# Two stages of a two-layer gated cross-attention program: normalised tiles turned by transposing DMAs in place of TensorE transposes

## The reference, cut to what matters

```python
def _layernorm(x, axis=-1, eps=1e-05):
    m = jnp.mean(x, axis=axis, keepdims=True)
    v = jnp.var(x, axis=axis, keepdims=True)
    return (x - m) / jnp.sqrt(v + eps)
```

## Time and profile before

| | us |
|---|---|
| runs | 2868.49, 2858.22, 2860.1 |
| median | 2860.1 |
| span of the profiled execution | 2840.7 |
| shared stage, within the span | 483 to 1000, about |
| last stage, within the span | 1995 to 2841, about |

### The profile page before, as it was taken

One profiled execution on the slowest core, in us unless ns is written; L12 is line 12 of the kernel. 1 busy time (PEld: TensorE's weight loads), 2 busy tenths in 40 slices (PEclk: granted clock), 3 DMA queues, 4 the chain that ended last, 5 costly groups with the idle time before them and its releaser, 6 DMA issues. The chain is left out here.

```text
span 2840.7 us, 47238 instructions
## 1 busy us (share of the span) xinstructions
PE 2697.2 (95%) x18014; PEld 1530.0 (54%) x18014; DVE 1632.8 (57%) x2693; ACT 1484.6 (52%) x3650; POOL 1042.2 (37%) x823
## 2 busy tenths in 40 slices
PE   6999988999999999999999989999999999999999
PEld 4555544444444467777777655566444444444444
DVE  7888885755555456655665478887633423333232
ACT  4888885333223256666666479999433222332221
POOL 2445452375455646666666401111102201220111
PEclk9999999999999999999999989999999999999999
DMA  4011104211111279999999710101400000000000
GB/s 156 21 55 50 50 16 146 67 46 49 49 49 35 75 253 293 273 289 287 283 288 293 177 60 31 61 31 50 144 34 1 30 30 30 1 30 30 15 1 30
DMA packets 152320, 277.75 MB, mean 98 GB/s; under 512 B 20000, under 2 KB 28960, under 8 KB 152096
## 3 DMA queue, kind: packets, MB, share of 16 engines
q1 hardware_dynamic: 115232, 207.39, 20.7%
q0 software_dynamic: 36864, 67.34, 11.2%
HBM read 198.86 MB, written 75.89 MB: 97 GB/s over the span
## 5 line engine op out<-in xcount | busy, mean ns | idle before, releaser
L1424 POOL DMA_INDIRECT ids<-sh_tk,sh_su x256 | 269.8, 1054 | 245.6 <-PE sh_gu L55 87.9
L55 PE MATMUL ex_gu<-ex_xT,ex_h 128*128 128x256 f16 x3072 | 347.3, 273 | 1.7 <-ACT ex_xT L1697 1.7
L55 PEld LDWEIGHTS ex_gu<-ex_xT,ex_h 128*128 128x128 f16 x3072 | 301.1, 98 | 51.0 <-ACT ex_xT L1697 1.9
L1829 POOL DMA_INDIRECT xp<-ex_oo,ex_to x128 | 241.8, 1889 | 177.5 <-ACT ex_oo L1731 136.3
L2408 POOL TENSOR_TENSOR fe_prodT<-fe_pp,fe_prodT 128x512 f16<-128x512 f32 x64 | 76.8, 1199 | 604.4 <-ACT fe_prodT L2175 604.4
L533 PE MATMUL at_g<-id,at_p 128*128 128x128 f32 x1280 | 211.8, 290 | 43.7 <-POOL at_p L928 23.7
L1555 DVE SCALAR_TENSOR_TENSOR ex_h<-ring,ex_h 128x1024 f16<-128x1024 f32 x128 | 151.1, 1222 | 151.6 <-ACT ex_h L1545 151.6
L533 PEld LDWEIGHTS at_g<-id,at_p 128*128 128x128 f32 x1280 | 165.6, 170 | 114.3 <-issue 46.7
L701 ACT ACTIVATE at_s<-at_s,at_mx 128x154 f32<-128x154 f32 x512 | 210.3, 416 | 0.0
L927 POOL TENSOR_TENSOR at_p<-at_s,at_rs 128x1024 f32<-128x1024 f32 x64 | 121.5, 1899 | 234.2 <-DVE at_rs L826 234.2
L2319 DVE SCALAR_TENSOR_TENSOR ring<-fe_g,fe_nf,ring 128x512 f32<-128x512 f32 x32 | 24.0, 751 | 293.1 <-PE fe_g L2079 293.1
(11 more groups left out here) (355 smaller groups left out, 5679.9 us busy)
## 6 DMA issues: line engine op xcount, KB each, us to landing
ring<-L_ffn_expert_gate_up_w SPq DMA_DIRECT2D x64, 1024.0 KB, 7.9
ring<-L_ffn_expert_down_w SPq DMA_DIRECT2D x64, 512.0 KB, 8.9
ring<-x SPq DMA_DIRECT2D x24, 1024.0 KB, 5.8
x<-ring SPq DMA_DIRECT2D x16, 1024.0 KB, 5.1
zrows<-hm_zs SPq DMA_DIRECT2D x32, 256.0 KB, 2.0
xp<-ring SPq DMA_DIRECT2D x8, 1024.0 KB, 5.1
out<-ring SPq DMA_DIRECT2D x8, 1024.0 KB, 4.2
ring<-xp SPq DMA_DIRECT2D x7, 1024.0 KB, 5.6
```

The lines of the kernel that those rows point to most:

```text
L55: mm = nc.tensor.matmul(out, lhs(a, k), rhs(b, k), start=start and i == 0 and j == 0, stop=stop and i == n - 1 and j == 2)
L1424: e.indirect_dma_start(ids, bass.IndirectOffsetOnAxis(slotu[b % 2][:, t, j:j + 1], 0), pair[b % 2][:, t, j, :], None, bounds_check=SLOTS - ...
L1829: e.indirect_dma_start(dst, bass.IndirectOffsetOnAxis(to[:, n:n + 1], 0), o32[y % 2][:, t, :], None, bounds_check=T + SLOTS - 1, oob_is_er ...
```

## The change

In the shared and the last stage, and for the four tiles that the first attention prepares for the shared stage, a DMA of SP's queue turns the tile: `sync_turn` waits for the low half and issues one transposing DMA from the buffer `zs` (128 rows by 2 x 512 values of 16 bits) straight into the tile's part of `zT`, both in SBUF. Its 8 TensorE transposes and the eviction by ScalarE or VectorE are gone, and so are the turns' PSUM banks. A buffer is free for the next high half when the DMAs of the tiles of its parity in the block before have landed (`hi_freed`). Whoever reads a block waits for 32 on each of two semaphores. The two attentions turn their own tiles as before. In SP's queue the turns of block b + 1 stand ahead of the stores to `zrows` of the same tiles; in the last stage behind the load of block b + 2 and ahead of the wait for block b's finished rows. Each has a wait on the last reader of the `zT` buffer ahead of it. The diff, cut to its core (the lines left out take the same turns out of ScalarE's and VectorE's loops, and name the new class in the last stage):

```diff
@@ -148,12 +148,15 @@
         v.tensor_scalar(self.z[n % 2][:, :], self.block(b)[:, t, :], self.mv[:, t, 0:1], self.rstd[:, t:t + 1],
                         ALU.subtract, ALU.mult).then_inc(s["z"], 1)
 
+    def hi_freed(self, n):
+        return self.s["turned"], n - self.nzs + 1
+
     def scalar_high(self, n):
 
         a, s = self.nc.scalar, self.s
         a.wait_ge(s["z"], n + 1)
         if n >= self.nzs:
-            a.wait_ge(s["turned"], n - self.nzs + 1)
+            a.wait_ge(*self.hi_freed(n))
         a.copy(self.zs[n % self.nzs][:, 0, :], self.z[n % 2][:, :]).then_inc(s["hi"], 1)
 
     def vector_low(self, n):
@@ -196,6 +199,37 @@
 
         self.nc.tensor.wait_ge(self.s["even"], 2 * b + 2)
         self.nc.tensor.wait_ge(self.s["odd"], 2 * b + 2)
+
+
+class QueueNorm(Norm):
+
+
+
+    def tile_out(self, n):
+        return super().tile_out(n).rearrange("p h k n -> p (h k) n")
+
+    def hi_freed(self, n):
+        return self.pair_turned(n // TPB - 1, n % 2)
+
+    def sync_turn(self, n):
+
+        e, s, slot = self.nc.sync, self.s, n % self.nzs
+        e.wait_ge(s["lo"], n + 1)
+        e.dma_start_transpose(self.tile_out(n), self.zs[slot][:, :, :].rearrange("p h d -> p (h d)")
+                              ).then_inc(s["odd" if n % 2 else "even"], 16)
+
+    def pair_turned(self, b, odd):
+
+        return self.s["odd" if odd else "even"], 32 * (b + 1)
+
+    def turned_all(self, engine, b):
+
+        for odd in range(2):
+            engine.wait_ge(*self.pair_turned(b, odd))
+
+    def tensor_block(self, b):
+
+        self.turned_all(self.nc.tensor, b)
 
 
 def place(h):
...
@@ -545,7 +579,7 @@
                     mm.then_inc(s["k_mm"], 1)
 
             def piece(what, B, k):
-                if what == "turn":
+                if what == "turn" and B < NB:
                     nm, _, n = whose(B, k)
                     nm.tensor_turn(n, bank(("turn", B, k), nm.turn_out(n)))
                 elif what == "project":
@@ -634,8 +668,6 @@
             if maps_ahead:
                 e.wait_ge(s["expd"], 2 * UNITS - 1)
                 maps_ahead.tensor_first()
-            if rows_ahead:
-                e.wait_ge(rows_ahead.s["turned"], TPB)
             e.wait_ge(s["f_mm"], TPB * NB)
 
         def scalar():
@@ -653,7 +685,7 @@
                                  ).then_inc(s["w_hi"], 1)
                 elif what == "prepare":
                     nm.scalar_high(n)
-                elif what == "turn" and n % 2 == 0:
+                elif what == "turn" and B < NB and n % 2 == 0:
                     if B:
                         e.wait_ge(s["q_mm"], KT * B)
                     nm.scalar_turned(n, bank_of["turn", B, k])
@@ -730,7 +762,6 @@
                 e.wait_ge(maps_ahead.s["w_hi"], 2)
             if rows_ahead:
                 e.wait_ge(rows_ahead.s["w_hi"], 3)
-                e.wait_ge(rows_ahead.s["even"], 2)
 
         def vector():
             e = nc.vector
@@ -754,7 +785,7 @@
                     nm.vector_z(n)
                 elif what == "low":
                     nm.vector_low(n)
-                elif what == "turn" and n % 2:
+                elif what == "turn" and B < NB and n % 2:
                     if B:
                         e.wait_ge(s["q_mm"], KT * B)
                     nm.vector_turned(n, bank_of["turn", B, k])
...
@@ -955,6 +985,10 @@
                     if L0:
                         e.wait_ge(s["lim_got"], B)
                         mask(B)
+                elif what == "turn" and B == NB:
+                    if k == 0:
+                        e.wait_ge(s["q_mm"], KT * B)
+                    rows_ahead.nrm.sync_turn(k)
                 elif what == "finish" and k == TPB - 1:
                     if rows_ahead and B == NB - 1:
                         rows_ahead.sync_next()
@@ -983,7 +1017,7 @@
             for what in plan[-1]:
                 piece(*what)
             for n in range(STEPS):
-                for what in plan[n]:
+                for what in sorted(plan[n], key=lambda what: what[0] != "turn"):
                     piece(*what)
 
         own_steps = count(1)
@@ -1008,7 +1042,7 @@
     def __init__(self, nc, ctx, K, I, ring, s, src, homes):
         self.nc, self.I, self.s, self.src, self.homes = nc, I, s, src, homes
         self.x = [ring[i] for i in (3, 2, 4, 1, 0)]
-        self.nrm = Norm(nc, ctx, "sh", s, K, self.x, homes)
+        self.nrm = QueueNorm(nc, ctx, "sh", s, K, self.x, homes)
         self.slots = [ring[i] for i in (4, 1, 0)]
 
         self.scat = [ctx.enter_context(nc.semaphore(f"sh_scat{i}")) for i in range(2)]
...
@@ -1172,8 +1201,6 @@
                     mm.then_inc(s["gu_mm"], 1)
                     if b == 0 and f == 3:
                         positions(0)
-                    for t in turning(b, f) if b + 1 < NB else ():
-                        turn((b + 1) * TPB + t)
                 if b + 1 < NB:
                     logits(b + 1)
                 if b == 0:
...
@@ -1460,7 +1468,10 @@
                 if b + 2 < NB:
                     rows(b + 2)
                 if b + 1 < NB:
+                    if b >= 1:
+                        e.wait_ge(s["gu_mm"], FB * b)
                     for t in range(TPB):
+                        nrm.sync_turn((b + 1) * TPB + t)
                         keep_rows((b + 1) * TPB + t)
                 else:
                     X.sync_ahead(H, ids)
@@ -1935,7 +1946,7 @@
         ps = lambda n, s_: ctx.enter_context(nc.psum_tensor(f"fe_{n}", s_, F32))
         gen = [F.gen[:, i, :] for i in range(2)]
         trio = [ps(f"p{i}", [P, 3, 512]) for i in range(2)]
-        nrm = Norm(nc, ctx, "fe", s, K, F.x, F.homes)
+        nrm = QueueNorm(nc, ctx, "fe", s, K, F.x, F.homes)
         nrm.zT.append(F.homes.a)
         left = [F.homes.b, sb("lf1", [P, 2, KT, KR], F16)]
         right = [sb(f"rt{i}", [P, 2, KT, KR], F16) for i in range(2)]
...
@@ -2080,9 +2088,6 @@
 
             for c in range(len(products)):
                 product(c)
-                if c in (5, 6):
-                    turn(2 * (c - 5))
-                    turn(2 * (c - 5) + 1)
             e.wait_ge(s["w_lo"], 2 * len(maps))
             out = bank(("c", NC), (s["c_lo"], NC + 1))
             split3(nc, out[:, :], lambda h, k: f0[:, h, k, 0:P], lambda h, k: wo[:, h, k, :], range(KT)
@@ -2101,8 +2106,6 @@
                     if b or j:
                         factors(b, j)
                     weigh(b, j)
-                    if nxt and 2 <= j < 2 + TPB:
-                        turn((b + 1) * TPB + j - 2)
                 if nxt:
                     hidden(b + 1)
                 last(b, 0)
...
@@ -2250,20 +2241,12 @@
                 e.wait_ge(own, next(own_steps))
                 e.tensor_scalar(nf[:, :], nf[:, :], K.tgw[:, 3:4], 1.0 / PS, ALU.mult, ALU.mult).then_inc(s["ready"], 1)
 
-            def turned(n):
-                b = n // TPB
-                if n % 2:
-                    if b >= 2:
-                        e.wait_ge(s["p_mm"], NJ * (b - 1))
-                    nrm.vector_turned(n, bank_of["turn", n])
-
             def running(b, k):
 
                 if k == 0:
                     if b >= 2:
                         e.wait_ge(s["cz_lo"], KT * (b - 1))
-                    e.wait_ge(s["even"], 2 * b + 2)
-                    e.wait_ge(s["odd"], 2 * b + 2)
+                    nrm.turned_all(e, b)
                     if b % NBB:
                         e.wait_ge(s["scan"], KT * b)
                 e.tensor_tensor_scan(cz[b % 2][:, k, :], nrm.turned(b)[:, 0, k, :], nrm.turned(b)[:, 1, k, :],
...
@@ -2418,6 +2396,10 @@
                 e.wait_ge(s["w_lo"], 2 * (n - 2))
                 F.sync_map(n)
 
+            def turns(b, tiles=range(TPB)):
+                for t in tiles:
+                    nrm.sync_turn(b * TPB + t)
+
             fetch(3)
             fetch(4)
             e.dma_start(r2[:, :, :], I["L1_ffn_router_w2T"].rearrange("(k p) m -> p k m", p=P)
@@ -2429,6 +2411,10 @@
             e.dma_start(alpha[:, :], row("alpha_bi", 1)).then_inc(s["small_in"], 16)
             for n in range(5, len(maps)):
                 fetch(n)
+                if n == 7:
+                    e.wait_ge(s["c_mm"], KT * 5)
+                    turns(0, range(2))
+            turns(0, range(2, TPB))
             for b, n in ((1, 9), (2, 7)):
                 e.wait_ge(s["w_lo"], 2 * n + 2)
                 nrm.sync_load(b, src)
@@ -2436,6 +2422,10 @@
                 if 1 <= b < NB - 2:
                     e.wait_ge(*stored(s, NX, b - 1))
                     nrm.sync_load(b + 2, src)
+                if b + 1 < NB:
+                    if b:
+                        e.wait_ge(s["p_mm"], NJ * b)
+                    turns(b + 1)
                 e.wait_ge(s["x_out"], TPB * b + TPB)
                 e.dma_start(dst[b * BLK:(b + 1) * BLK, :].rearrange("(t p) d -> p t d", p=P),
                             nrm.block(b)[:, :, :]).then_inc(s[f"st{b % NX}"], 16)
```

(20 more changed lines are left out.)

## The result

| | before | after |
|---|---|---|
| median of four runs each, us | 2859.16 | 2829.4 |
| lowest to highest, us | 2857.23 to 2868.49 | 2827.3 to 2831.88 |

The ratio is 0.9899 (95% interval 0.9878 to 0.9921): 29.8 us, 1.0%, faster. The profiled execution of the changed kernel took 2831.88 us and spans 2830.1 us, so 1.8 us lie outside a span. The same difference shows in every run whose time and span are both on record.

What follows compares the result with a forecast made beforehand. TensorE's instruction stream was taken to bound both stages; 17.9 + 12.5 + 4.1 = 34.5 us leave it and the DMAs cost nothing, so 2860.1 - 34.5 gives 2826 us, range 2818 to 2862 us.

Steps and rivals of the forecast that it cites:

- Shared stage, 17.9 us: TensorE's turns and their waits leave the shared stage: 14.7 us in blocks 1 to 6, 3.2 us in block 0.
- The block's 25.90 us: Shared stage, step f=3 to the next block's logits: five steps of 5.18 us remain of 28.35 us.
- Last stage, 12.5 + 4.1 us: 28 turns of 0.45 us leave TensorE, 12.5 us; bank waits in the weight products ahead go, 4.1 us.
- First attention, 0 (up to 1.8) us: Four turns leave TensorE, but no single engine bounds this stage; counted 0, with 1.8 us of gain as bound.
- Evictions, nothing: The 64 evictions by ScalarE and VectorE were hidden under TensorE; removing them is worth nothing in itself.
- L: Time from the end of a tile's low half to its landing by DMA; taken as 4.6 us, between 2.0 and 7.2.
- Deadlines: Longest L without cost: 7.2 us before the shared stage's logits, about 5.6 us before the last stage's running sums.
- the named wait: Last stage, TensorE's 0.51 us wait for ScalarE's gelu; grows 1 us a block per microsecond of L above 5.6.
- Rival 2, queueing: DMA turns one tile at a time, slower than low halves come; at 6.2 us each the gain is gone; chance 0.21.
- The base: Savings found in the 2840.7 us profiled span were subtracted from the 2860.1 us median, 19.4 us above it.

Runs made afterwards that it cites:

- e2_last_only: Changed kernel with TensorE's turns restored in the shared stage and first attention, only the last stage turning by DMA; 2818.24 us, ratio 0.9944 to the kernel before.
- dead turns: Changed kernel in which TensorE still makes its 56 turns in both stages, into banks nobody reads; 2848.19 us, ratio 0.9973 to the kernel before.
- e1_after: The changed kernel, unedited, profiled a second time; 2800.3 us against 2835.22 us for the kernel before, ratio 0.9877.
- e8_before: The kernel before, unedited, run once more with a profile; 2853.85 us, ratio 1.0012.
- e9_after: The changed kernel, unedited, run again against the kernel before on the same chip; 2827.51 us against 2853.68 us, ratio 0.9909.

## Why the prediction was right, point by point

2826 us was forecast, 2829.4 us measured; in the gain 34.5 us against 29.8 us in the first comparison, 34.9 us on chip P and 26.2 us on chip R. The mechanism held everywhere, what leaves TensorE's stream is saved; the size held in full on chip P alone. Elsewhere the gain is 5 to 8 us short, by something for which the prediction had no term.

- **Shared stage, 17.9 us.** 16.6 us on chip P (532.6 - 516.0). The block's 25.90 us came out to the hundredth; 1.1 us went into the one new wait for VectorE. On chip R the term is 8.0 us, and no step of the prediction had that.
- **Last stage, 12.5 + 4.1 us.** 12.5 and 4.1 us in all three pairs, within 0.1 us.
- **First attention, 0 (up to 1.8) us.** 1.5 us on chip P, not separable from the spread between profiles: 482.4 to 484.2 us in the three of the kernel before, 480.1 us in e2_last_only, which is the same there, and 477.3 to 480.9 us where the DMAs turn the four tiles. So it may also be more than 1.8 us.
- **Evictions, nothing.** Held in the last stage (dead turns: 716.6 us); not settled in the shared stage.
- **L, taken as 4.6 us.** It is 2.7 us. That cost the forecast nothing, but partly by luck: in block 0 of the shared stage only 3.45 us are free, so with 4.6 us TensorE would have waited there for 1.2 us (an estimate from the rows of e1_after). The middle between 2.0 and 7.2 us was too far up: the nearer row was the plain store, which lands in 2.0 us before and, with a median of 2.4 us in e1_after, behind the transposing DMA. By the Trainium skill, "Advanced Engine Details and Errata", section X-Bar Transpose (TRN2), the two kinds should be equally fast; the trace agrees roughly, at 2.7 against 2.4 us. The Trainium skill's page "VectorE: DVE Perf Modes", section The three transpose paths, gives 1309 ns for one 128x128 block; eight in 2.7 us disagree with that as a rate. The same page of the Trainium skill advises TensorE where PSUM will do (section Rules for kernel authors); following it costs 1.2% here (34.9 of 2835 us on chip P), where TensorE is the bound.
- **Deadlines.** In the last stage a tile is free at 5.1 us, as forecast; at 8.4 us most of the cost sat in the named wait, and it was 11.2 us, not 20. The shared stage's 7.2 us holds for block 1 (6.8 us in e1_after), not for block 0 (3.45 us).
- **Rival 2, queueing.** In the loops tiles mostly follow each other at 5.2 us and more (block 0 of the shared stage has two at 2.6 us), and each lands after 2.7 us; it would have needed twice that. The argument that no row of 256 KB needs more than 7.2 us was a wrong reading: single loads of that size take up to 8.1 us in the same trace.
- **The base.** The prediction saw the median 19.4 us above the span and wrote "I let that difference stand". It should not have stood: only 1.8 us lie outside a span. The rest goes, as far as these runs tell, with the chip or the time of measuring. The shown profile of before has the 532.6 us shared stage of chip P, while its shown times are nearer to those of chips Q and R (2855 and 2854 us). A base profile like that of e8_before would have shown the gaps beforehand, though not that they would grow. This is where the last 4.7 us of the first comparison most likely went; its own profile has 539.9 us in the shared stage, as on chip R.

## What to carry to other kernels

Where TensorE's stream sets the end and the DMA engines are idle (share 0.16 and 0.08), turning a tile by a transposing DMA was worth the TensorE time that it removed, as the tile was wanted later than 2.7 us after it was written; on the chips with gaps part of it was lost again. Find the deadline in the timeline, not at the first reader alone but at the engine that has no slack behind it, and in every block: the first block has another order, and here it had half the free time of the next. Compare the span with the times before using a profile as a base: here a span and its own run are 1.8 us apart, and 19.4 us meant that profile and times were of different conditions.

## What the runs showed of the hardware

- A transposing DMA of 256 KB from SBUF to SBUF held SP for 1.24 us (2.2 us at most) and landed in 2.7 us at the median (4.5 us at most), in packets under 512 B: with the 64 of them the page counts 87584 such packets, without them 20000.
- The same kernel took 2835 us on chip P, 2855 on Q, 2854 on R, each measured at one time. From P to R 15.3 us of it lie in the shared stage, where TensorE, VectorE and ScalarE show waits with no releaser in the trace.
- Such gaps weigh more after the change (9.2 us idle and clock 0.95, from 5.4 us and 0.98, on chip R).
- TensorE was slow after such a gap: idle for half of 590 to 600 us, it then had a granted clock of 0.52 for 5 us, and the same 48 matmuls took 12.9 in place of 10.5 us (e9_after).
